# Sums of a wide attention step in a bank of a ring of four, added in SBUF by VectorE

## The reference

```python
# wide (L0, L2)
q, k, v = x @ Wq, ctx @ Wk, ctx @ Wv                  # 16 heads of 64
logits = einsum(q, k) * 64 ** -0.5
logits += -20 * (1 - mask_A) at token_indices_A, -20 * (1 - mask_B) at token_indices_B
x = softmax(logits) @ v @ Wo + bo + x
# narrow (L1, L3)
xn = x * rsqrt(mean(x * x) + 1e-5) * norm_w
x = x + softmax(einsum(xn @ wq, ctx @ wk) * 16 ** -0.5) @ (ctx @ wv) @ wo
```

## Time and profile before

| | |
|---|---|
| median of 3 runs | 1754.18 us (1751.69 to 1755.21) |
| profiled execution | 1748.67 us |
| its span, mean granted clock | 1746.9 us, 0.968 |
| preparation, until the layers' first instructions | about 192 us |
| HBM read, written | 115.11 MB, 43.48 MB |

### The profile page before, as it was taken

The page is one execution under the profiler, slowest core; times in us unless marked ns, Lnnn a source line. Parts: engine busy times, 40 slices in busy tenths (PEclk is TensorE's granted clock), DMA queues, the critical chain, the costliest instruction groups (busy, mean ns, idle before and its releaser), DMA issues.

```text
span 1746.9 us, 29686 instructions
## 1 busy us (share of the span) xinstructions
PE 1617.9 (93%) x10732; PEld 882.6 (51%) x10732; DVE 1197.9 (69%) x2313; ACT 1023.9 (59%) x1737; POOL 471.9 (27%) x353
## 2 busy tenths in 40 slices
PE   7998698999999999999999999899999999999794
PEld 6886444444545454544545454445454545454442
DVE  5474547676777687768777777678777877775551
ACT  2111165666667676767666766576676767676452
POOL 5342402123222231223131313132322322232212
PEclk9898898999999999999999999999999999999986
DMA  7998402151315121512353323412151325131422
GB/s 255 323 317 242 140 25 58 37 98 28 84 32 132 27 78 27 131 35 80 69 115 91 73 54 80 91 40 72 41 122 27 82 41 125 26 81 23 123 69 81
DMA packets 176738, 160.57 MB, mean 92 GB/s; under 512 B 91722, under 2 KB 133066, under 8 KB 175570
## 3 DMA queue, kind: packets, MB, share of 16 engines
q1 hardware_dynamic: 174578, 150.29, 33.5%
q10 hardware_dynamic: 2016, 8.39, 1.2%
HBM read 115.11 MB, written 43.48 MB: 91 GB/s over the span
## 4 chain that ended last, share of the span: by engine, by line
PE 46%; issue 16%; DVE 10%; POOL 7%; ACT 3%; SPq 3%; DMA 3%; POOLq 0%; ACTq 0%; DVEq 0%
PE general L1649 9%; PE general L1528 7%; POOL kept L1402 4%; PE score_ps L1587 4%; PE score_ps L1588 4%; PE out_ps L1605 4%; PE general L1545 3%; PE general L1549 3%; PE score_ps L1576 2%; PE out_ps L1625 2%; DVE q_pair L1440 2%; DVE q_aux L1439 2%; SPq L1135 2%; DVE q_pair L1441 2%; PE general L1669 2%
## 5 line engine op out<-in xcount | busy, mean ns | idle before, releaser
L1451 DVE TENSOR_REDUCE tops<-general 128x2 bf16<-128x308 f32 x1024 | 433.2, 470 | 88.1 <-PE general L1545 40.1
L1292 ACT ACTIVATE probs<-score_ps 128x512 f32<-128x512 f32 x512 | 297.7, 598 | 141.0 <-PE score_ps L1588 128.0
L1402 POOL TENSOR_TENSOR kept<-kept,inv_b 128x512 f32<-128x512 f32 x128 | 170.7, 1355 | 464.9 <-DMA inv_b<-scratch_inverses 464.9
L1438 DVE CAST q_aux<-q_pair 64x512 bf16<-64x512 f32 x160 | 74.8, 468 | 194.1 <-ACT q_pair L1280 192.9
L1304 ACT ACTIVATE q_aux<-general 4x512 bf16<-4x512 bf16 x320 | 187.5, 586 | 31.7 <-PE general L1558 26.1
L1279 ACT ACTIVATE q_pair<-general 64x512 fp32r<-64x512 f32 x160 | 94.6, 591 | 156.7 <-PE general L1528 156.1
L1545 PE MATMUL general<-w_top,q_aux 128*128 128x154 bf16 x1024 | 133.4, 237 | 36.5 <-DVE q_pair L1441 26.1
L1341 ACT ACTIVATE a_hi<-kept 128x512 fp32r<-128x512 f32 x160 | 93.6, 624 | 112.0 <-POOL kept L1402 48.1
L1464 DVE TENSOR_TENSOR a_lo<-kept,a_hi 128x512 fp32r<-128x512 f32 x160 | 123.9, 807 | 49.7 <-ACT a_hi L1341 48.9
L1392 POOL TENSOR_TENSOR x_lo<-xn,x_hi 128x1024 fp32r<-128x1024 f32 x31 | 73.6, 2375 | 285.0 <-ACT x_hi L1260 145.6
L1588 PE MATMUL score_ps<-q_pair,w_pair 128*128 128x512 f32 x256 | 149.4, 589 | 0.0
(11 more groups left out here) (157 smaller groups left out, 3305.7 us busy)
## 6 DMA issues: line engine op xcount, KB each, us to landing
inv_b<-scratch_inverses SPq DMA_DIRECT2D x128, 256.0 KB, 4.8
w_pair<-scratch_wk_hi SPq DMA_DIRECT2D x32, 256.0 KB, 4.9
x<-scratch_stream SPq DMA_DIRECT2D x16, 512.0 KB, 3.3
inv_n<-scratch_inverses SPq DMA_DIRECT2D x256, 32.0 KB, 1.9
xn<-scratch_stream SPq DMA_DIRECT2D x15, 512.0 KB, 3.4
scratch_stream<-x SPq DMA_DIRECT2D x14, 512.0 KB, 4.9
scratch_wk_hi<-p_kout_hi SPq DMA_DIRECT2D x16, 308.0 KB
p_raw<-in_L_xattn_Wk_dram SPq DMA_DIRECT2D x4, 1024.0 KB, 7.8
```

Of the source, the lines that this page charges most:

```text
L1292: nc.scalar.activation(dst, score_ps[:, number % 2, :], ACT.Exp, scale=scale).then_inc(act_exp.sem, 1)
L1402: last = nc.gpsimd.tensor_tensor(tiles[i], tiles[i], (inv_b, inv_n)[n % 2][:, i, :], ALU.mult)
L1451: last = nc.vector.tensor_reduce(tops[:, n % 2, sub, 2 * pair:2 * pair + 2], src, AX_X, ALU.max)
```

## The change

1. The ring has four banks instead of three; `sum_ps` goes. Value 1 of a wide step takes a use of the ring for its sums (before its sums matmuls it waits for the use four before); every step's sums start anew. VectorE copies them to `wide_sums` in SBUF in steps 0 and 8 and adds them in the others, in the list's place of value 1, and is the reader of that bank. ScalarE's copy goes; TensorE doesn't wait for it any more before value 0 of steps 0 and 8; SP's store of the sums waits for the last addition.
2. VectorE takes the low part of a query before it casts.
3. In `prepare` the norm weights of both pairs have their own place and are loaded right after piece 1.
4. At the start of `layers` GpSimd clears `q_aux[:, 0]` first of all, not VectorE. ScalarE issues the loads of the key rows for the maxima and the first mask rows (four transfers) ahead of its list, not SP.

The list of entries is the same.

```diff
-GB = 3
+GB = 4
...
-GENERAL = [(*x, m) for x in PLAN if x[1] in ("query", "max", "turn", "output", "square", "rate", "give")
+WIDE_STEPS = [n for n in range(STEPS) if wide(n)]
+GENERAL = [(*x, m) for x in PLAN if x[1] == "value" and x[2] in WIDE_STEPS and x[3] == 1 or x[1] in ("query", "max", "turn", "output", "square", "rate", "give")
            for m in range(KC if x[1] == "output" else 1)]
...
-        sum_ps = ctx.enter_context(nc.psum_tensor("sum_ps", [P, 512], F32))
...
-        act_sums = Signal(sem("act_sums"), ("sums",), only=(0, 2))
+        dve_sums = Signal(sem("dve_sums"), ("value",), only=WIDE_STEPS, parts=(1,))
...
-        reader = {"query": dve_query, "max": dve_max, "turn": act_turn, "output": dve_output,
+        reader = {"value": dve_sums, "query": dve_query, "max": dve_max, "turn": act_turn, "output": dve_output,
...
                         if c % 2 == 0:
-                            wait(sp, act_sums.sem, act_sums.after(w, what, c, 0))
+                            wait(sp, dve_sums.sem, dve_sums.after(w, "value", 4 * c + 3, 1))
                             sp.dma_start(dr["sums"], wide_sums[0:P:8]).then_inc(sums_stored.sem, 32)
...
             sp.wait_ge(rows_cleared, 1)
             load_wide_keys(0, 0, 0)
-            load_top_rows(0)
-            sp.wait_ge(rows_cleared, 2)
-            load_masks(0)
-            sp.wait_ge(rows_cleared, 4)
+            sp.wait_ge(rows_cleared, 3)
             load_aux_rows(0)
...
         @block.scalar
         def _(act):
+            act.wait_ge(rows_cleared, 1)
+            load_top_rows(act, 0)
+            act.wait_ge(first_cleared, 1)
+            load_masks(act, 0)
+
...
-                elif what == "sums":
-
-                    if n % 2 == 0:
-                        wait(act, pe_value.sem, pe_value.after(it, "value", 4 * n + 3, 1))
-                        wait(act, sums_stored.sem, sums_stored.after(it - (n == 0), what, 2 - n, 0))
-                        nc.scalar.activation(wide_sums[:], sum_ps[:], ACT.Copy).then_inc(act_sums.sem, 1)
...
         @block.gpsimd
         def _(pool):
+            nc.gpsimd.memset(q_aux[:, 0].bitcast(F32), 0.0).then_inc(first_cleared, 1)
...
         @block.vector
         def _(dve):
-            for buf in (w_top[:], q_aux[:, 0], w_aux[:], w_aux_rest[:], tops[:]):
+            for buf in (w_top[:], w_aux[:], w_aux_rest[:], tops[:]):
                 nc.vector.memset(buf.bitcast(F32), 0.0).then_inc(rows_cleared, 1)
...
-                    nc.vector.tensor_copy(q_aux[0:64, t, s, j, :], q_pair[0:64, s, j, :])
-                    nc.vector.tensor_copy(q_aux[64:P, t, s, j + 1, :], q_pair[64:P, s, j + 1, :]).then_inc(dve_aux.sem, 1)
                     nc.vector.tensor_tensor(q_pair[64:P, s, j, :], ps[0:64], q_pair[0:64, s, j, :], ALU.subtract)
                     last = nc.vector.tensor_tensor(q_pair[0:64, s, j + 1, :], ps[64:P], q_pair[64:P, s, j + 1, :], ALU.subtract)
                     last.then_inc(dve_query.sem, 1)
+                    nc.vector.tensor_copy(q_aux[0:64, t, s, j, :], q_pair[0:64, s, j, :])
+                    nc.vector.tensor_copy(q_aux[64:P, t, s, j + 1, :], q_pair[64:P, s, j + 1, :]).then_inc(dve_aux.sem, 1)
...
+                elif what == "value":
+
+                    if not wide(n) or k == 0:
+                        return
+                    wait(dve, pe_value.sem, pe_value.after(it, what, n, k))
+                    ps = bank_of((it, what, n, k, 0))
+                    if n % 4 == 0:
+                        wait(dve, sums_stored.sem, sums_stored.after(it - (n == 0), "sums", 2 - n // 4, 0))
+                        nc.vector.tensor_copy(wide_sums[:], ps).then_inc(dve_sums.sem, 1)
+                    else:
+                        wait(dve, dve_sums.sem, dve_sums.after(it, what, n - 1, 1))
+                        nc.vector.tensor_tensor(wide_sums[:], ps, wide_sums[:], ALU.add).then_inc(dve_sums.sem, 1)
...
-                    if n in (0, 8) and k == 0:
-
-                        wait(pe, act_sums.sem, act_sums.after(it - (n == 0), "sums", 2 - n // 4, 0))
...
                         if k == 1:
+                            sum_ps = bank((it, what, n, k, 0))
                             for j in range(4):
                                 nc.tensor.matmul(sum_ps[SUMS[j]], sel[:, g, :], probs[:, j, :],
-                                                 start=(g == 0), stop=False, skip_group_check=True)
+                                                 start=True, stop=False, skip_group_check=True)
```

In `prepare`:

```diff
-        normw = sb("p_normw", [P, KC])
+        normw = sb("p_normw", [P, 2, KC])
...
-                if name == "nq":
-                    if p:
-                        sp.wait_ge(s_hi, len(pieces) // 2)
-                    sp.dma_start(normw[:, :], ins[f"L{2 * p + 1}_xattn_norm_w"].rearrange("(k p) -> p k", p=P)).then_inc(s_nw, 16)
...
                 load_piece(1)
+                for p in range(2):
+                    sp.dma_start(normw[:, p, :], ins[f"L{2 * p + 1}_xattn_norm_w"].rearrange("(k p) -> p k", p=P)).then_inc(s_nw, 16)
```

More of the change, by code:

```diff
@@ L411, in _ @@
                 if name == "nq":
-                    act.wait_ge(s_nw, 16 * (p + 1))
+                    act.wait_ge(s_nw, 16 * 2)
                     for k in range(KC):
                         nc.scalar.activation(view(raw, i)[:, k], view(raw, i)[:, k], ACT.Copy,
-                                             scale=normw[:, k:k + 1]).then_inc(s_evh, 1)
+                                             scale=normw[:, p, k:k + 1]).then_inc(s_evh, 1)
                     act.wait_ge(s_evh, KC * (p + 1))
@@ L840, with __init__ @@
 class Signal:
-    def __init__(self, sem, kinds, times=1, only=range(STEPS)):
+    def __init__(self, sem, kinds, times=1, only=range(STEPS), parts=range(8)):
         self.sem, self.times = sem, times
@@ L846, in __init__ @@
         for w, what, n, k in PLAN:
-            if what in kinds and n in only:
+            if what in kinds and n in only and k in parts:
                 made += times
@@ L925, in layers @@
         cleared = sem("cleared")
-        rows_cleared = sem("rows_cleared")
+        rows_cleared, first_cleared = sem("rows_cleared"), sem("first_cleared")
         filled, rows_filled = sem("filled"), sem("rows_filled")
@@ L982, in last_query, with rows_of, load_top_rows, load_masks @@
             return (before_w, "query", 4 * before + 3, 1) if before % 2 == 0 else (before_w, "query", 4 * before + 2, 0)
+        def rows_of(buf, par):
+            a = 64 * (1 - par)
+            return buf[a:a + 6].rearrange("p (h two) k -> p h two k", two=2)[:, :, par, :]
+        def load_top_rows(eng, p):
+            for par in range(2):
+                eng.dma_start(rows_of(w_top, par), dr["keyrows"][p][:, None, :].to_broadcast([6, 8, KEYS])).then_inc(top_rows_loaded, 16)
+        def load_masks(eng, t):
+            for par in range(2):
+                a = 64 * (1 - par)
+                eng.dma_start(q_aux[a:a + 6, t].rearrange("p s (j two) n -> p (s j) two n", two=2)[:, :, par, :],
+                             dr["maskrows"][t][:, None, :].to_broadcast([6, 4, TOK])).then_inc(masks_loaded[t], 16)
         def bank_of(use):
@@ L992, in load_wide_query @@
                     sp.dma_start(wq[i][:, :, at:to].bitcast(F32), dr["wq_" + a][p, :, :, at:to]).then_inc(wide_query_loaded, 16)
[L994 to L1002, removed]
             def load_aux_rows(p):
@@ L1103, in load_early @@
                 sp.dma_start(xn[:], dr["stream"][bass.ds(b, 1), t].rearrange("o p k n -> p (o k) n")).then_inc(early_loaded.sem, 16)
[L1105 to L1110, removed]
             def store_x(c, w, b):
@@ L1228, in each_entry @@
                             if w == B:
-                                load_top_rows(1)
+                                load_top_rows(sp, 1)
                                 load_aux_rows(1)
@@ L1242, in _ @@
             sp.wait_ge(cleared, 1)
-            load_masks(1)
+            load_masks(sp, 1)
             load_x(0, 0)
@@ L1295, in do @@
                     if (it, n) == (0, 0):
-                        act.wait_ge(rows_cleared, 2)
+                        act.wait_ge(first_cleared, 1)
                     if (it, n) == (0, 8):
@@ L1619, in do @@
                                 last = nc.tensor.matmul(sum_ps[SUMS[j]], sel_rest[rows, g, :], rest[rows],
-                                                        start=False, stop=(g == 3), skip_group_check=True)
+                                                        start=False, stop=True, skip_group_check=True)
                     else:
```

4 lines of the change are left out of this document (3 added, 1 removed).

## The result

| | before | changed |
|---|---|---|
| median of 20 runs | 1749.20 us (1744.47 to 1756.10) | 1756.85 us (1749.69 to 1764.82) |
| profiled execution, span, clock | 1748.67, 1746.9, 0.968 | 1749.69, 1747.7, 0.971 |
| ratio | | 1.0046 [1.0031, 1.0060] |

The changed kernel is slower by 0.46%, some 8 us. The time before was 1754.18 in the three runs shown ahead; over 20 runs its median is 1749.20, and the ratio is to that. The profiled execution of the changed kernel happens to be the fastest of its 20, 7 us under their median, and only 1 us above the profiled one of before.

What follows compares the result with a forecast made beforehand. TensorE was taken to bound the kernel, VectorE to pace reductions in narrow stretches. Terms +9.7 - 14.7 + 1.4 - 1.1 - 0.5 - 1.5 gave -6.7, so 1754.2 became 1747.5 us; 8 in 10 range 1730 to 1765.

Steps and rivals of the forecast that it cites:

- Part 1: VectorE's additions of the sums delay the rate chain from query 3 0 to 4 0 by 0.69 us, 14 times: +9.7 us.
- Part 2: Fourth ring bank in the narrow stretches: net relief of 2.1 us a window, seven times, -14.7 us.
- The bank: TensorE's 24 waits a window for VectorE's reductions, 0.13 us each, go: 3.1 us gained in a window.
- The additions at the heads of the narrow stretches: Additions at value 3 1 and value 11 1 meet a VectorE without gaps: 1.4 us given back in a window.
- The third: Low part first frees a query's bank sooner, for the load of max 13 6: 0.4 us gained in a window.
- The 0.13 us for a wait: Score to next max on TensorE takes 0.45 us without a bank wait, 0.58 with one; a wait costs 0.13.
- Part 3: Casts come 1.38 us later; value matmuls cover that except at max 8 0 of the first window: +1.4 us.
- Parts 4 and 5: Start: clearing moved to GpSimd, first transfers to ScalarE, -1.1 us; norm weights loaded first, -0.5 us.
- The sum: All terms together, last window's -1.5 us included: -6.7 us, median 1747.5 us.
- (c): Slower: additions before max 5 3, 13 5 join pacing VectorE, ring useless; sign query 8 0 later; +17.7, 1772; chance 0.22.
- (a): The ring gives its upper bound, 5.4 us in a window: -29.8 us, 1724; chance 0.15.
- (d): VectorE is the bound throughout, all 64 copies and additions on the path: +44.1 us, 1798; chance 0.03.

Runs made afterwards that it cites:

- e3: The changed kernel with the old order of a query put back (casts first, low part last); ratio to before 0.9957, median 1743.73 us.
- e6: As e3, but a ring of three banks and the sums in a bank of their own, VectorE still adding; ratio to before 1.0086, 1764.65 us.
- e7: As e3, but nobody reads the sums: no copy or addition by VectorE, a constant instead; ratio to before 0.9905, 1733.12 us.
- e12: The kernel before with the low part first only in the wide queries; ratio to before 1.0004, median 1751.74 us.
- e2: The kernel before with only the order of a query changed (low part first, casts last); ratio to before 1.0069, median 1765.07 us.
- e9: As e8, with the low part of a query first; ratio to before 0.9802, median 1713.81 us.
- e8: The kernel before with GpSimd's work on kept cut to 8 of 512 columns; ratio to before 0.9774, median 1709.38 us.

## Why the prediction was wrong, point by point

- **Part 1, additions in the chain: right.** 9.7 us forecast for it. It grew by 0.60 us in each window, not 0.69, since the next instruction starts before the addition's recorded end. Putting the addition behind the multiplication gave 6.5 us back, so the loss was where the prediction put it.
- **Part 2, the ring: the balance right, in part by luck.** It has three terms. The bank was to give 3.1 in a window and 1.5 at the end, 23 us; e3 against e6 gives 23, but e7 only 17, where 25 was forecast (23, and 1.6 for the start). The additions at the heads of the narrow stretches were to take 1.4 in a window, 9.8 us beside the 9.7 of part 1, so 19.5 for all; measured were 9 with four banks and 14 with three. So with four banks these heads cost nothing that shows, and two terms that were too large cancelled. The third, 0.4 in a window for the low part first, belongs to part 3. The working was wrong too: under 8 of 24 waits for the reductions were to stay, and 17 stayed. The 0.13 us for a wait was the difference of two places that can't be compared, matmuls of a wide max and weight loads of a narrow one.
- **Part 3, the cast last: this step failed.** It said that a block of value matmuls covers the casts, and that only max 8 0 of the first window pays, 1.4 us; part 2 even booked 0.4 in a window as a gain, 2.8 us. Measured: 12 us lost alone, 16 in the changed kernel. Max 8 0 did pay what was forecast (its wait rose from 2.18 to 3.60), and the cover exists: e12, with the wide queries alone, costs nothing that shows. Two things were missing. The casts were taken to be only later, by 1.38 us, and as short as the 0.42 of the earlier trace rows, while the groups had a mean of 468 and 564 ns, so some take much longer. Which ones depends on what GpSimd does at that moment, and the order decides it: the two casts of query 6 0 took 0.84 us in every window of e3 and 1.9 to 3.7 in the changed kernel. And I asked only who waits for the casts, not what stands behind them on VectorE. That is the maxima, in stretches which the earlier trace rows show as VectorE's. The load of max 13 6 did come sooner with the low part first, but the net is a loss.
- **Parts 4 and 5, start and norm weights:** 1.6 us faster forecast, 1.0007 [0.9991, 1.0023] measured. No gain is shown; 1.6 us is at the edge of the interval.
- **The sum** without part 3 and its 2.8 was -5.3 us; e3, which is that kernel, measured -7.5. Part 3 turned -7.5 into +8. That -5.3 and -7.5 are so near is the luck of part 2.
- **The rivals.** The result lies on the side of (c), slower, but its mechanism was another: (c) had the addition in front of max 5 3 and max 13 5 as the cause and the ring as useless, and e3 and e7 speak against both. Its sign came, query 8 0 later behind its stretch (122.4 us against 116.5 over seven windows), but with the additions and the casts first the stretch is shorter than before, 113.3. What (c) had right is that VectorE sets the pace there. (a) and (d) fell. That the additions would lengthen the kernel by up to 44 us, as the prediction drew from the busy shares by the rule of the Trainium skill (Perfetto Trace Analysis, Identifying the Most-Contended Engine), was not borne out: 9 (4 to 14).

Not settled: where the 2 to 7 us of the price lie that the stretch from query 6 0 to query 8 0 doesn't hold, what the end of ScalarE's copies gave, and why the profiled executions of e2 and of the changed kernel, each under its median by 9 and 7 us, show only a part of the loss.

## What to carry to other kernels

When instructions swap places on an engine, their cost isn't only who waits for the last of them: look at what another engine does at the new moment, since a VectorE cast from SBUF to SBUF took 0.42 us alone and 0.89 to 1.04 on average beside GpSimd, while a subtraction out of PSUM didn't mind. A mean in the groups that lies above the duration in the timeline (564 against 420 ns) was the sign here that such meetings exist. And what a step delays is first of all the queue behind it on its own engine; here that cost nothing in the stretches where TensorE was the pace (e12), and nearly all of it where VectorE was (query 6 0 to query 8 0). Being late cost nothing there; being long did (e9).

## What the hardware showed unexpectedly

- GpSimd's jobs cost this kernel more than their share of 27% suggests: cutting 247 us of them (471.9 to 224.7) made it 40 us faster (e8). VectorE's casts fell by 28 us and its subtractions of `a_lo`, which read both operands from SBUF, from 123.9 to 104.1 us:

```profile
L1464 DVE TENSOR_TENSOR a_lo<-kept,a_hi 128x512 fp32r<-128x512 f32 x160 | 104.1, 683 | 23.8 <-ACT a_hi L1341 22.5
```

  How much of the 40 us is contention and how much an earlier output was not separated.
- VectorE started its next instruction before the recorded end of the one ahead: behind the start of an addition recorded with 0.69 us, the next came after 0.61 (590.07 to 590.68).
